# Spreading the MLP's steps over all 32 rounds of a tile, and adding seven rounds' halves on VectorE

## What is computed

```python
e = jnp.stack([tbl_0[ids[:, 0]], tbl_1[ids[:, 1]], ...], axis=1)      # 2048 x 32 x 64
p, q = e[:, ids_x, :], e[:, ids_y, :]                                # 496 pairs
pw = jnp.einsum('bpi,pij->bpj', p, w)
z = jnp.einsum('bpj,bpj->bp', pw, q)                                 # 2048 x 496
h = jnp.concatenate([z, dense_ctx], axis=1)                          # 2048 x 512
h = jnp.maximum(h @ W_top1 + b_top1, 0.0)                            # 512
h = jnp.maximum(h @ W_top2 + b_top2, 0.0)                            # 256
y = h @ W_top3                                                       # 1
```

## Time and profile before

| | us |
|---|---|
| three runs, median (lowest, highest) | 956.79 (955.41 to 956.92) |
| profiled execution, its own time | 953.77 |
| its span, first to last instruction | 952.0 |
| PE busy | 794.7 (83%) |
| DVE busy | 594.2 (62%) |
| POOL busy | 590.5 (62%) |
| ACT busy | 196.0 (21%) |

### The profile page before, as it was taken

The page is one execution under the profiler, slowest core; times in us unless marked ns, Lnnn a source line. Parts: engine busy times, 40 slices in busy tenths (PEclk is TensorE's granted clock), DMA queues, the critical chain, the costliest instruction groups (busy, mean ns, idle before and its releaser), DMA issues.

```text
span 952.0 us, 10237 instructions
## 1 busy us (share of the span) xinstructions
PE 794.7 (83%) x3792; PEld 285.4 (30%) x3792; DVE 594.2 (62%) x512; ACT 196.0 (21%) x333; POOL 590.5 (62%) x612
## 2 busy tenths in 40 slices
PE   0444958988696999999697999999698799999969
PEld 0111213333232333333232333333233233333313
DVE  0132638976595576777585566688586566689930
ACT  1221212211222122211221222211131222210001
POOL 6756775687687566777577467677577567641110
PEclk9967779999799999999799899999799999999979
DMA  7113449998797577999697478888798578886970
GB/s 280 26 41 67 110 89 218 216 200 198 154 231 172 122 154 167 196 198 200 144 229 175 93 160 184 179 192 199 160 217 186 118 161 183 178 175 135 193 160 0
DMA packets 40760, 153.78 MB, mean 162 GB/s; under 512 B 11332, under 2 KB 11716, under 8 KB 28296
## 3 DMA queue, kind: packets, MB, share of 16 engines
q0 software_dynamic: 30208, 117.48, 62.3%
q1 hardware_dynamic: 10504, 35.67, 10.6%
HBM read 52.43 MB, written 0.01 MB: 55 GB/s over the span
## 4 chain that ended last, share of the span: by engine, by line
PE 61%; issue 10%; another core or an unknown queue 9%; POOL 7%; DMA 6%; DVE 4%; ACT 2%; DVEq 0%; POOLq 0%
PE main_ps L329 34%; PE z_ps L353 13%; PE x_ps L384 7%; DMA prod<-prod 6%; POOL emb L233 5%; DVE prod L417 4%; PE x_ps L309 2%; PE main_ps L384 2%; ACT quad_t L451 2%; POOL prod L245 2%; PE main_ps L330 1%; ACT e_t L440 0%; ACT L440 0%; DVEq L154 0%
## 5 line engine op out<-in xcount | busy, mean ns | idle before, releaser
L417 DVE TENSOR_TENSOR prod<-main_ps,quad_t 128x1024 f32<-128x1024 f32 x448 | 522.6, 1217 | 204.5 <-PE main_ps L330 118.0
L233 POOL DMA_INDIRECT emb<-in_tbl,idx x512 | 496.2, 969 | 198.4 <-issue 150.5
L329 PE MATMUL main_ps<-e_t,w_sb 64*128 64x512 f32 x1024 | 500.4, 625 | 91.4 <-DVE prod L417 44.9
L330 PE MATMUL main_ps<-e_t,w_sb 64*128 64x512 f32 x1024 | 500.3, 625 | 0.0
L329 PEld LDWEIGHTS main_ps<-e_t,w_sb 64*128 64x128 f32 x1024 | 184.7, 193 | 360.3 <-issue 227.4
L353 PE MATMUL z_ps<-prod,const_sb 128*32 128x512 f32 x1280 | 175.1, 639 | 28.7 <-DMA prod<-prod 21.9
L330 PEld LDWEIGHTS main_ps<-e_t,w_sb 64*128 64x128 f32 x1024 | 184.8, 193 | 0.0
L245 POOL DMA_DIRECT2D prod<-prod x96 | 94.2, 985 | 126.2 <-DVE prod L417 119.8
L417 DVE TENSOR_TENSOR prod<-main_ps,e_t 128x1024 f32<-128x1024 f32 x64 | 78.1, 1220 | 115.1 <-PE main_ps L330 81.6
L451 ACT ACTIVATE quad_t<-x_ps 32x512 f32<-32x512 f32 x224 | 131.4, 587 | 2.6
L440 ACT ACTIVATE e_t<-x_ps 128x512 f32<-128x512 f32 x64 | 38.3, 598 | 431.8 <-PE x_ps L309 195.9
(11 more groups left out here) (11 smaller groups left out, 24.6 us busy)
## 6 DMA issues: line engine op xcount, KB each, us to landing
prod<-prod POOLq DMA_DIRECT2D x96, 1024.0 KB
w_sb<-in_w SPq DMA_DIRECT2D x65, 512.0 KB
emb<-in_tbl,idx POOLq DMA_INDIRECT x512
w_sb<-in_w SPq DMA_DIRECT2D x1, 1024.0 KB
z_sb<-in_ctx SPq DMA_DIRECT2D x64, 2.0 KB
idx<-in_ids SPq DMA_DIRECT2D x1, 192.0 KB
const_sb<-in_const SPq DMA_DIRECT2D x1, 125.0 KB, 2.0
idx<-in_ids SPq DMA_DIRECT2D x1, 64.0 KB, 2.0
```

Source lines behind the costliest of these rows:

```text
L233: pool.indirect_dma_start(out=emb[:, n % G_SLOTS, s, odd * EMBED:(odd + 1) * EMBED], out_offset=None, in_=tables[f], in_offset=bass.Indire ...
L329: nc.tensor.matmul(main_ps[:, slot, :], w_sb[LOW, u % W_SLOTS, :], even[LOW, 0, :], start=True, stop=True)
L330: nc.tensor.matmul(main_ps[:, slot + 1, :], w_sb[UP, u % W_SLOTS, :], odd[UP, 0, :], start=True, stop=True)\
L417: nc.vector.tensor_tensor(prod[:, s:s + 2, :], main_ps[:, slot:slot + 2, :], e_q, ALU.mult)\
```

## The change

The MLP's seven steps stand in front of rounds 6, 10, 14, 18, 20, 26 and 30, not 4, 6, 8, 10, 12, 14 and 16. `z_sb` gets a second buffer, since a tile's first copy of z (in round 10) now comes before the MLP has read the last one (until round 18). In the seven rounds just ahead of those, 5, 9, 13, 17, 19, 25 and 29, DVE adds the halves, as its first instruction of the following round; 17 of the 24 sums stay with the DMA. This holds for all four tiles, though the first has no MLP steps among its rounds.

```diff
-DMA_FOLDS = FULL
-DVE_FOLDS = []
...
-MLP_ROUNDS = (4, 6, 8, 10, 12, 14, 16)
+MLP_ROUNDS = (6, 10, 14, 18, 20, 26, 30)
+
+DVE_FOLDS = [r for r in FULL if r + 1 in MLP_ROUNDS]
+DMA_FOLDS = [r for r in FULL if r not in DVE_FOLDS]
...
-        z_sb = sb("z_sb", [P, KTILES, TILE])
+        z_sb = sb("z_sb", [P, 2, KTILES, TILE])
...
-                    w, x, m = w1_sb, z_sb, n
+                    w, x, m = w1_sb, z_sb[:, t % 2], n
...
+                    if u % ROUND == 0 and n > 0 and (u // ROUND - 1) % ROUNDS in DVE_FOLDS:
+
+                        dve.wait_ge(products, n)
+                        s = 2 * ((n - ROUND) % P_SLOTS)
+                        low, high = prod[:, s:s + ROUND, :], prod[:, s + ROUND:s + 2 * ROUND, :]
+                        nc.vector.tensor_tensor(low, low, high, ALU.add).then_inc(folded, 1)
                     dve.wait_ge(mains, n + 1)
...
-                if kt == 0 and t > 0:
-                    act.wait_ge(mlp_ps, MLP_STEPS * (t - 1) + HID1 // P)
-                nc.scalar.activation(z_sb[:, kt, :], z_ps[:, :], ACT.Copy).then_inc(z_out, 1)
+                if kt == 0 and t > 1:
+
+                    act.wait_ge(mlp_ps, MLP_STEPS * (t - 2) + HID1 // P)
+                nc.scalar.activation(z_sb[:, t % 2, kt, :], z_ps[:, :], ACT.Copy).then_inc(z_out, 1)
```

More of the change, by code:

```diff
@@ L292, in _ @@
                     for row, f in CTX_ROWS[n]:
-                        sp.dma_start(z_sb[row:row + 1, n, :], ctx_t[f:f + 1, t * TILE:(t + 1) * TILE]).then_inc(ctx_in, 16)
+                        sp.dma_start(z_sb[row:row + 1, t % 2, n, :], ctx_t[f:f + 1, t * TILE:(t + 1) * TILE]).then_inc(ctx_in, 16)
                 elif kind == "mlp" and n == MLP_STEPS - 1:
@@ L418, in _ @@
                       .then_inc(products, 1)
-                    if u % ROUND == 1 and n >= ROUND and (u // ROUND - 1) % ROUNDS in DVE_FOLDS:
-                        dve.wait_ge(products, n - 1)
-                        s = 2 * ((n - ROUND - 1) % P_SLOTS)
-                        low, high = prod[:, s:s + ROUND, :], prod[:, s + ROUND:s + 2 * ROUND, :]
-                        nc.vector.tensor_tensor(low, low, high, ALU.add).then_inc(folded, 1)
-            if ROUNDS - 1 in DVE_FOLDS:
-                dve.wait_ge(products, NUNIT * TILES)
-                s = 2 * ((NUNIT * TILES - ROUND) % P_SLOTS)
-                low, high = prod[:, s:s + ROUND, :], prod[:, s + ROUND:s + 2 * ROUND, :]
-                nc.vector.tensor_tensor(low, low, high, ALU.add).then_inc(folded, 1)
         @block.scalar
```

## The result

The changed kernel takes **959.39 us** in the median of 20 runs (955.25 to 970.6), the kernel before 954.6 in as many (948.81 to 960.69) on the same chip. The ratio is 1.0058, with an interval of 1.0034 to 1.0082: slower by 0.6%. A few executions are over 1.5% longer than the fastest of their kernel; the ratios in this document leave them out, the medians don't. The forecast was 899 us and faster, with 884 to 941 as its range.

A forecast was written before the change was run, and what follows sets the result against it. PE was taken as the bound all through after the change. 29.2, tiles of 248, 194, 194, 190.5 and tail 38.1 make 893.8 us; 1.8 outside the span and 3.0 to the median give 899, range 885 to 915 (8 in 10: 884 to 941).

The forecast's parts named there:

- slow stretches: Rounds 2 and 3 and 23 to 25 of tile 1, 8.5 and 13.4 us over PE's need; PE completes late.
- the slow stretches go with their cause: With POOL no longer falling behind, tiles 1 and 2 approach 190.0 us, taken as 194, from 216.6 each.
- POOL is the slowest engine: Step-free rounds 17 to 22 and 26 to 1: POOL 6.16 us between DMA sums, PE and DVE 4.93 a round.
- rival, in which the stretches stay: The slow stretches have another cause and stay in tiles 1 to 3; about 16 us gained, 940 us; chance 18%.
- The 21.9 us: Kernel before: PE waits 13 times for sums to land, 21.9 us in all; well under that expected after.
- POOL for the other 19: Each tile is uneven: PE sets the pace for 13 rounds, POOL for the other 19.
- three cases in which the stretches stay: Stretches stay, 940 us, 18%; nothing changes, 956 us, 5%; slower, past 956.8 us, 8%.
- slower: Runs of plain rounds each set off a stretch, 13.4 us at worst; one more in three tiles makes 980; 8%.
- PE's terms: PE per tile: 16 pairs at 9.85, 8 unfolded at 0.87, 7 steps at 3.63, 190.0 us; tile 3 187.1.
- The cover of round 29: Where PE makes a step DVE idles 3.65 us, so a 2.4 us sum is covered with 1.2 left.
- VectorE's sums: Seven a tile, 28 in all, 2.4 us each on DVE; they cost nothing in tiles 1 to 3.
- POOL is held up by DVE's sum: A gather stands still for each DVE sum, POOL losing 2.4 us 28 times; 920 us; chance 12%.
- Tile 0: POOL-bound from round 13; five sums fewer there, 6 us off, 248; PE running three units ahead hides most uncovered sums.

The follow-up runs named there:

- schedule alone: Changed kernel with all sums left to DMAs, against the kernel before: 878.69 us (0.9769), 932.05 us (0.9887) and 933.65 us (0.9894) on three chips.
- second group: Runs on one chip: kernel before 940.59 us, changed kernel 948.98, changed with round 29 by DMA 942.65, schedule alone 932.05.
- runs with covered sums: Schedule alone with DVE's sums before the six full steps of tiles 1 to 3, 18 in all: ratios 1.0055 and 1.0038 to the kernel before.

## Why the prediction was wrong

**The step that failed** is "the slow stretches go with their cause": that PE is late there because it waits for sums that fall behind, since "POOL is the slowest engine" ahead of both. By the prediction's own rival, in which the stretches stay, 16 of the 58 us are left without it; so it carried 42. GpSimd was late, and the change made it less late. The rest was refuted three ways. With GpSimd's sums at most 3.6 us behind, tile 1 loses 25.8 us in four stretches, where it lost 22 in two; with no DMA sum to wait for a tile takes 220.0; with GpSimd's gathers gone it takes 187.9. What stands in the step's place is a late completion on PE that comes only where GpSimd gathers.

The trace of the kernel before could have told most of it. The 21.9 us of the earlier trace rows are of the whole span, 8.7 of them in the tail. In tile 1 alone, 283.0 to 499.6, PE's waits for sums are:

```profile
PE z_ps L353 <- DMA prod<-prod: 3.8, 2, 2.1
```

That is 3.8 of 26.6 us (0.9 in tile 2), and landing records are missing from this trace, so it may be somewhat low; all idle time of PE ahead of L353 is 6.8 in tile 1. "POOL for the other 19" rounds was a misreading too: rounds 26 to 30 take 6.07, 4.63, 5.22, 4.63 and 5.22 us, PE's own terms, while the sums fall 4.6 us behind, and the 9.85 itself was read in such a run. And the 14 us of lateness in round 0 of tile 0 come ahead of the first sum. I had two things standing close together, a lag and a late PE, and took the first for the cause. The prediction's own words, that the trace shows the work completing late and doesn't show why, should have weighed more than the 31% for the three cases in which the stretches stay.

**The rival that came closest** is "slower": stretches in more places, of the shorter runs that the new order makes (15 to 17, 21 to 25 and 31 to 5 were on its list; rounds 10 and 11 lie between two of its entries, and 7 to 9 and 27 to 29 stayed without one). Its price was too high. The new stretches of tile 1 took 4.7 and 4.3 us and not 13.4; of the old ones the second fell from 13.4 to 5.6, and that of rounds 2 and 3 grew from 8.5 to 11.2. So it ends at 959 and not 980. Its condition, "PE, DVE and the DMAs are all near full", doesn't fit: with plain loads the DMAs are busy for 0.93 and no stretch comes, without sums for 0.24 and the tile is longest. With GpSimd's gathers in the DMAs' place it fits tiles 1 to 3, and the start of tile 0 has a late completion without PE or DVE near full.

**PE's terms** were right but one. Pairs, reduces, full steps and missing transposes hold; the last step doesn't. Its round lasts 6.33 us and a plain one 4.63 (timeline of DVE, schedule alone, rounds 29 and 30 of tile 1):

```profile
444.28 4.62 DVE L424 TENSOR_TENSOR prod<-main_ps,quad_t 128x1024 f32<-128x1024 f32 x4 [0.60 <-PE main_ps L331]
450.61 4.62 DVE L424 TENSOR_TENSOR prod<-main_ps,quad_t 128x1024 f32<-128x1024 f32 x4 [1.71 <-PE main_ps L331]
```

So it is 1.7 us, for 3.63 in the sum, and the floor is 188.1 by the terms; 187.9 was measured. The 13.55 us that I read for rounds 15 and 16 are 6.33 and 7.23, so round 16 held a small slow stretch of 2.0.

**The cover of round 29** fell with that term: the sum takes 2.29 us there, and the step 1.7. In tiles 1 to 3 of the changed kernel the round takes 6.86 us, which is the step and 0.53 more (timeline of DVE, changed kernel, tile 1):

```profile
493.12 4.62 DVE L424 TENSOR_TENSOR prod<-main_ps,quad_t 128x1024 f32<-128x1024 f32 x4 [0.60 <-PE main_ps L331]
497.77 2.29 DVE L409 TENSOR_TENSOR prod<-prod 128x2048 f32<-128x2048 f32 x1
499.98 4.61 DVE L424 TENSOR_TENSOR prod<-main_ps,quad_t 128x1024 f32<-128x1024 f32 x4
```

**VectorE's sums.** Their size was right: 2.29 us for 2.4. "It costs nothing in tiles 1 to 3" was wrong, by 0.4 to 0.75 us each where a step covers them. One effect of them is seen directly. Timelines of GpSimd and of DVE, changed kernel, round 5 of tile 1:

```profile
337.20 0.95 POOL L234 DMA_INDIRECT emb<-in_tbl,idx  x1 [0.30 <-issue]
338.46 2.22 POOL L234 DMA_INDIRECT emb<-in_tbl,idx  x1 [0.30 <-issue]
340.98 0.95 POOL L234 DMA_INDIRECT emb<-in_tbl,idx  x1 [0.30 <-issue]
```

```profile
337.55 2.29 DVE L409 TENSOR_TENSOR prod<-prod 128x2048 f32<-128x2048 f32 x1
```

The gather that starts while the sum runs ends at 340.68, 0.84 us after the sum's end at 339.84; the one that had begun before it isn't touched. Over the span a gather takes 1030 ns for 969 before (groups by line, changed kernel, then kernel before):

```profile
L234 POOL DMA_INDIRECT emb<-in_tbl,idx x512 | 527.2, 1030 | 202.6 <-issue 145.2 <-DVE prod L424 33.0 <-remote 13.6
```

```profile
L233 POOL DMA_INDIRECT emb<-in_tbl,idx x512 | 496.2, 969 | 198.4 <-issue 150.5 <-DVE prod L417 25.7 <-remote 14.2
```

31 us over 28 sums are 1.1 us for each, against 1.0 us of issue that each saves GpSimd: nothing is won there. So the rival "POOL is held up by DVE's sum" happened with half its price; what it cost in time no run separates. By the first half of the rule cited from the Trainium skill ("SBUF — State Buffer", "Who interferes with whom"), that the one that starts later blocks fully, the trace agrees: 2.22 us for 0.95. The second half, the inference that descriptor generation (GpSimd's writing out of a DMA's transfers) isn't caught, can be read in the kernel with 18 additions that nobody waits for, where sums' issues too start inside an addition (timelines of DVE and GpSimd):

```profile
422.30 1.76 DVE L417 TENSOR_TENSOR scratch<-w_sb 128x1536 f32<-128x1536 f32 x1
```

```profile
422.87 1.01 POOL L248 DMA_DIRECT2D prod<-prod  x1
```

All ten such issues of a DMA sum take 0.84 to 1.02 us, none held up, so the inference holds for them. The eight gathers that start inside one take 1.41 to 2.38, each ending 0.82 after it. A gather's issue reads its indices (`idx`) from SBUF and a sum's has none to read, which would fit the first half; no run shows that this is what sets them apart.

**Tile 0** was to win 6 us and lost 12.2 in the profiled run (7.8 against the schedule alone in the second group: 264.1 and 256.3 us from the first product to tile 1). What "up to three units that PE may run ahead hide" did not happen: in the profiled run of the changed kernel its rounds 9, 13, 17, 25 and 29 last 6.9 us, as a round with an uncovered sum does. Against the kernel before, where round 17 took 7.18 anyway, these five add 4.4 us of the 12.2; 5.6 lie ahead of round 13, where the forecast saw no change, and aren't explained.

**What holds of the change.** By the medians the schedule is worth 8.5 us at 940 and 21 us at 900; VectorE's sums take back about 17 at 940. The version that beats both kernels is the schedule with all sums by DMA: 0.9887 where the changed kernel has 1.0078, 0.9894 in a third group, and 0.9769 on the fastest chip.

**What stays open.** Why PE completes late while GpSimd gathers isn't settled. In tiles 1 to 3 it needs the gathers and doesn't come with plain loads from SyncE, and it differs by chip: this is shown. That it grows when DVE does more rests on the runs with covered sums and added additions, that it is longest without DMA sums on one execution. A mechanism that joins them isn't shown. Plain loads issued by GpSimd in the gathers' place weren't tried; nor was the changed kernel run on the 900 us chip. The split of VectorE's 17 us between covered sums (7 to 13) and the ten uncovered ones is a difference of medians from different chips, so rough.

## What to carry to other kernels

A lag and a stall that stand side by side are not yet cause and effect: ask which began first, and whether the stall also comes where the lag isn't; one kernel that removes the suspected work altogether would have told it, and so would the first 60 us of the trace, where the stall stood ahead of any sum. A wait should be added up in the stretch that it is to explain, not over the span. A rest that the sum over rounds doesn't explain should be forecast to stay, perhaps elsewhere, until its cause is known. And work moved to an engine with idle time is not free: here covered sums cost 0.4 to 0.75 us apiece, while another engine's issues were held up and PE finished later in the rounds behind them.

## What was unexpected of the hardware

The same program takes 899.7 us on one chip and 938 to 955 on others, at a granted clock of about 0.97 and 0.94. For the schedule-only kernel the spans are 877.5 and 934.1, 56.6 us apart. 38.5 of them lie in tiles 1 to 3, in the slow stretches, and 13.7 in round 0 of tile 0, with the late completion shown above. Without the gathers of tiles 1 to 3 the two chips are alike: the schedule-only kernel has 187.9 us in tile 2 on a chip with 940, and the changed kernel 188.3 on the one with 900.

On the slower chips the trace holds fewer landing records: 476 for the first gather buffer of the schedule-only kernel (second group), for 1368 on the fast one, from the same DMAs. "Remote" as a releaser comes with that, and waits for a landing are undercounted: PE's waits for sums add up to 20.7 us there, for 50.7 on the fast chip, whose tiles are shorter.

Late completions and missing records come together; whether one brings the other, no run here tells.
